# One GpSimd power for the squares of one group and the variances of another, in a macaron block on one core

## The reference

```python
x = x + 0.5 * ffn(layernorm(x), w_up, w_down)
x = x + attn(layernorm(x), Wf, Wi, Wh)
x = x + 0.5 * ffn(layernorm(x), w_up, w_down)

def ternary_linear(x, w):
    alpha = mean(abs(w))
    w_t = sign(w) * (abs(w) > 0.5 * alpha)
    x_norm = x / (sqrt(sum(x * x)) / sqrt(d) + 1e-8)
    return x_norm @ w_t.T

ffn  = ternary_linear(gelu(ternary_linear(x, w_up)), w_down)      # 128 -> 512 -> 128
attn = h, with h[t] = sigmoid(Wf x[t]) * h[t-1] + sigmoid(Wi x[t]) * g(Wh x[t])   # written with logarithms
```

## Time and profile before

| What | Value |
|---|---|
| median of 3 runs | 262.69 us (262.29 to 263.86) |
| the profiled execution | 263.04 us |
| its span, first to last instruction | 261.3 us |
| mean granted TensorE clock | 0.991 of full speed |
| TensorE matmul busy | 236.6 us (91%) |
| VectorE busy | 234.1 us (90%) |
| ScalarE busy | 221.4 us (85%) |
| GpSimd busy | 216.4 us (83%) |
| DMA, over the span | 9.73 MB, mean 37 GB/s |

### The profile page before, as it was taken

One profiled execution on the slowest core, in us unless ns is written; L12 is line 12 of the kernel. 1 busy time (PEld: TensorE's weight loads), 2 busy tenths in 40 slices (PEclk: granted clock), 3 DMA queues, 4 the chain that ended last, 5 costly groups with the idle time before them and its releaser, 6 DMA issues.

```text
span 261.3 us, 9753 instructions
## 1 busy us (share of the span) xinstructions
PE 236.6 (91%) x3759; PEld 167.1 (64%) x3759; DVE 234.1 (90%) x754; ACT 221.4 (85%) x534; POOL 216.4 (83%) x400
## 2 busy tenths in 40 slices
PE   0759999999998899899999998679999999999992
PEld 0626777777777667655555544357777776777782
DVE  3798799999999998999999999986999999988784
ACT  2377999989998899879999997997899999999861
POOL 5676998989998898599999999998889989997133
PEclk9988999999999999999999999999999999999999
DMA  6990000000000000000000000000111211112114
GB/s 188 300 265 3 4 4 3 3 3 4 3 3 4 3 4 4 3 0 1 3 1 0 0 1 3 3 3 3 43 43 57 67 46 43 43 43 82 46 43 123
DMA packets 18062, 9.73 MB, mean 37 GB/s; under 512 B 608, under 2 KB 17888, under 8 KB 18016
## 3 DMA queue, kind: packets, MB, share of 16 engines
q1 hardware_dynamic: 17744, 8.98, 12.5%
q10 hardware_dynamic: 272, 0.13, 0.2%
HBM read 4.92 MB, written 4.19 MB: 35 GB/s over the span
## 4 chain that ended last, share of the span: by engine, by line
PE 53%; DVE 21%; ACT 7%; POOL 7%; issue 6%; DVEq 0%; ACTq 0%; POOLq 0%
PE Y L502 17%; PE U L458 9%; PE G L489 9%; PE U L459 8%; DVE hidden L701 5%; PE T L439 4%; ACT h_hi L330 4%; DVE st L719 3%; DVE h_lo L654 3%; PE U L518 2%; DVE cand L691 2%; DVE mv L619 2%; PE G L478 2%; POOL xn L236 2%; POOL root L212 2%
## 5 line engine op out<-in xcount | busy, mean ns | idle before, releaser
L654 DVE SCALAR_TENSOR_TENSOR h_lo<-h_hi,U 128x1024 f16<-128x1024 f16 x63 | 75.6, 1215 | 10.0 <-ACT h_hi L330 9.6
L324 ACT ACTIVATE U<-U 128x1024 f32<-128x1024 f32 x63 | 64.7, 1026 | 15.3 <-PE U L459 14.4
L236 POOL TENSOR_SCALAR xn<-X,neg_mean,rstd 128x128 f32<-128x128 f32 x156 | 67.8, 447 | 6.9 <-DVE rstd L624 4.2
L330 ACT ACTIVATE h_hi<-U 128x1024 f16<-128x1024 f32 x63 | 64.7, 1027 | 1.0
L502 PE MATMUL Y<-down_w,h_hi 128*128 128x128 f16 x496 | 59.4, 220 | 0.0
L502 PE MATMUL Y<-down_w_half,h_lo 128*128 128x128 f16 x496 | 59.0, 219 | 0.0
L458 PE MATMUL U<-xt_hi,up_w 128*128 128x512 f16 x128 | 49.2, 384 | 9.4 <-DVE h_lo L654 7.5
L212 POOL TENSOR_TENSOR root<-mv,half 128x8 f32<-128x8 f32 x31 | 51.0, 1644 | 2.3
L459 PE MATMUL U<-xt_lo,up_w 128*128 128x512 f16 x128 | 49.2, 384 | 0.0
L502 PEld LDWEIGHTS Y<-down_w_half,h_lo 128*128 128x128 f16 x496 | 48.5, 98 | 0.4
L502 PEld LDWEIGHTS Y<-down_w,h_hi 128*128 128x128 f16 x496 | 47.7, 98 | 1.6
(11 more groups left out here) (101 smaller groups left out, 415.2 us busy)
## 6 DMA issues: line engine op xcount, KB each, us to landing
X<-in_L_attn_x SPq DMA_DIRECT2D x16, 256.0 KB, 5.3
out_x<-X SPq DMA_DIRECT2D x15, 256.0 KB, 2.8
up_raw<-in_L_ffn_w_up SPq DMA_DIRECT2D x1, 256.0 KB, 4.5
down_raw<-in_L_ffn_w_down SPq DMA_DIRECT2D x1, 256.0 KB, 4.7
out_x<-X SPq DMA_DIRECT2D x1, 128.0 KB, 1.9
out_x<-X ACTq DMA_DIRECT2D x1, 128.0 KB, 2.9
gate_raw<-in_L_attn_Wh SPq DMA_DIRECT2D x1, 64.0 KB, 3.7
gate_raw<-in_L_attn_Wi SPq DMA_DIRECT2D x1, 64.0 KB, 3.6
```

The costliest lines, as they stand in the source:

```text
L236: m = eng.tensor_scalar(xn[:, n % 2, t, :], X[:, c, :], neg_mean[l][:, c:c + 1], rstd[l][:, c:c + 1], ALU.add, ALU.mult)
L324: eng.activation(U[part][:], U[part][:], ACT.Gelu, scale=1.0 / XN_SPLIT).then_inc(gelu_done, 1)
L330: eng.mul(h_hi[:, F % 2, 2 * part:2 * part + 2, :], U[part][:], H_SPLIT).then_inc(h_hi_done, 1)
L654: vec.scalar_tensor_tensor(out=h_lo[:, F % 2, 2 * part:2 * part + 2, :], in0=h_hi[:, F % 2, 2 * part:2 * part + 2, :], scalar=-1.0 / H_SPL ...
```

## The change

- **One power.** Where turn F of a feed-forward block still has a group five ahead of it (F + 5 in the same block), the sum of squares of F is written beside the variances of that group (`mv` column 3, already scaled by 4 / 512), and one GpSimd power takes all 12 values a partition (`ln_roots`); one addition makes both denominators (the floor of the fourth column is set once), and one reciprocal on VectorE both factors (`scale`). `rms_step`, `y_scale` and their instructions remain for the last five turns of either block.
- **Order on GpSimd and VectorE.** GpSimd's `ln_roots` of group k + 3 now stands before `norm` of k + 2, and the moments (`mv` column 2, `neg_mean`) before that, at the end of the turn before. VectorE's reciprocal stands between the two `h_lo` of turn k and takes group k + 3; statistics of group k + 4 stand after the adds.
- **Head.** Normalizing group 0 stands before the first weight limits; statistics of group 3, a first `h_lo` and the second ternary step are put in another order.
- **First turn's gates.** The gates of the first two turns of the recurrence stand before the gram and down of the last group, in other PSUM banks; the sum of squares of group 14 goes to VectorE; four tiles of statistics are taken out there and done in four later turns of five.
- **Start of the second feed-forward block.** The last add of the recurrence stands before the statistics.
- **End.** The last gram is done by columns between the rows of the down product before; the last adds wait for two rows of the down product at a time; the rows added by GpSimd are shared with VectorE, and their output goes in two DMAs.

The diff, cut to what the text speaks of:

```diff
+        def rides_with(F):
+            l, k = (0, F) if F < groups else (2, F - groups)
+            return (l, k + 5) if k + 5 < groups else None
+
+        def rider(l, g):
+            return None if g < 5 else g - 5 if l == 0 else g - 5 + groups
...
             def ln_roots(l, g):
-                if l == 0 or g >= BY_ACT:
-                    ln_moments(l, g)
+                F = rider(l, g)
+                w = 2 if F is None else 3
                 pool.wait_ge(var_set[l], 2 * (g if l == 0 else g + 1))
-                eng.tensor_tensor(root[l][:, g % 2], mv[l][:, cols(g), 1:3], half[:], ALU.pow).then_inc(root_done[l], 1)
+                if F is not None:
+                    pool.wait_ge(ssq_done, F + 1)
+                eng.tensor_tensor(root[l][:, g % 2, :, 0:w], mv[l][:, cols(g), 1:1 + w], half[:, :, 0:w],
+                                  ALU.pow).then_inc(root_done[l], 1)
...
+                if 2 <= k < groups - 3:
+                    ln_roots(0, k + 3)
+                elif groups - 3 <= k < groups:
                     rms_step(k - 2)
...
-                if k + 3 < groups:
-                    ln_roots(0, k + 3)
-                if 0 <= s - 28 < groups:
+                if k + 4 < groups:
+                    ln_moments(0, k + 4)
+                if 0 <= s - 28 < BY_ACT:
                     ln_roots(2, s - 28)
+                if 0 <= q < groups - 4:
+                    ln_moments(2, q + 4)
...
             def scales(l, g):
                 dve.wait_ge(den_done[l], g if l == 0 else g + 1)
-                vec.reciprocal(rstd[l][:, cols(g)], den[l][:, g % 2]).then_inc(rstd_done[l], 1)
+                if rider(l, g) is None:
+                    vec.reciprocal(scale[l][:, cols(g), 0], den[l][:, g % 2, :, 0]).then_inc(rstd_done[l], 1)
+                else:
+                    vec.reciprocal(scale[l][:, cols(g), :], den[l][:, g % 2]).then_inc(rstd_done[l], 1)
...
+            for k in range(2, groups):
+                if k + 1 < groups:
+                    low_part(k + 1)
+                if k == 2:
+                    scales(0, 4)
                 h_low(k, 0)
+                if 2 < k < groups - 3:
+                    scales(0, k + 3)
                 h_low(k, 1)
+                if k == 2:
+                    scales(0, 5)
+                if diagonal_by_max(k - 1):
+                    sum_squares(k - 1)
+                finish_ffn(k - 2)
+                if k + 4 < groups:
+                    stats(0, k + 4)
+                    mean_var(0, k + 4)
+                if k == groups - 1:
+                    candidate(0)
+                later_stats(k)
...
-                room = 0 if s < groups - 9 else 1 if s < groups - 5 else 4
+                room = 0 if s < groups - 9 else 1 if s < groups - 5 else 5 if groups + 3 <= s < groups + 7 else 4
...
+            turn(groups + 1)
+            for n in range(3):
+                gate(0, n)
+            gate(1, 0)
+            turn(groups + 2)
+            gate(1, 1)
+            gate(1, 2)
+            gram(groups - 1)
+            down(groups - 1)
+            turn_back(0)
...
+            down(LAST - 1, [0])
+            last_gram(0)
+            last_gram(1)
+            last_gram(2)
+            down(LAST - 1, [1])
+            last_gram(3)
+            down(LAST - 1, [2, 3])
+            down(LAST)
```

More of the change, by code:

```diff
@@ L145, in cols, with rstd, y_factor, y_ready @@
             return slice(g * TILES, g * TILES + n)
+        def rides_with(F):
[3 more added lines that the diff above has]
+            return None if g < 5 else g - 5 if l == 0 else g - 5 + groups
+        alone = [F for F in range(2 * groups) if not rides_with(F)]
+        def rstd(l, c):
+            return rstd1[:, c:c + 1] if l == 1 else scale[l][:, c, 0:1]
+        def y_factor(F, t):
+            if not rides_with(F):
+                return y_scale[:, F % 4, t:t + 1]
+            l, g = rides_with(F)
+            return scale[l][:, g * TILES + t, 1:2]
+        def y_ready(engine, F):
+            if rides_with(F):
+                l, g = rides_with(F)
+                engine.wait_ge(rstd_done[l], g + 1)
+            else:
+                engine.wait_ge(y_scale_done, alone.index(F) + 1)
         def by_both(n):
@@ L491, in gram, with products @@
-                m.then_inc(gram_done, 1)
+            def products(F, t, c, last):
+                for right in (h_hi, h_lo):
+                    for n in range(2):
+                        e = slice(t * P + n * HALF, t * P + (n + 1) * HALF)
+                        m = pe.matmul(gram_of(F)[n * HALF:(n + 1) * HALF, t, 0:HALF], h_hi[:, F % 2, c, e], right[:, F % 2, c, e],
+                                      start=False, stop=last and right is h_lo, tile_position=(0, n * HALF))
+                return m
@@ L493, in down, with last_gram @@
+            def last_gram(c):
+                pe.wait_ge(h_lo_done, 2 * LAST + max(c, 1))
+                if c == 0:
+                    mask(LAST)
+                for t in range(TILES):
+                    m = products(LAST, t, c, t == TILES - 1 and c == chunks - 1)
+                if c == chunks - 1:
+                    m.then_inc(gram_done, 1)
             def down(F, rows=range(TILES)):
@@ L771, in _ @@
+            scan(0)
+            candidate(1)
+            finish_ffn(groups - 2)
+            later_stats(groups + 1)
+            scan(1)
+            add_rnn(0)
+            finish_ffn(groups - 1)
+            candidate(2)
+            later_stats(groups + 2)
+            add_rnn(1)
+            for s in range(groups + 3, 2 * groups):
+                r = s - groups
                 if r == groups - 1:
                     low_part(groups)
[L773 to L774 removed]
```

348 lines of the change are left out of this document (206 added, 142 removed).

## The result

The changed kernel takes **271.13 us** (median of 4 runs, 270.70 to 271.72); the kernel before, beside it, 262.62 (262.29 to 263.86). The ratio is 1.0317, 95% interval [1.0283, 1.0352]: slower by 3.2%. The forecast was 270.6 us, with 264.3 to 275.0 as the range. The profiled execution took 271.72 us, with a span of 269.4 (before 263.04 and 261.3).

The account below looks back on a forecast made before the run. Several engines at once held a feed-forward turn, with TensorE's floor at 5.35 us; the new loop would exceed it. Terms summed to +7.95 on 263.04, 270.99, less 0.35 to the median: 270.6 us, range 264.3 to 275.

Parts of the forecast that it names:

- The loop: First feed-forward block: mv, power, reciprocal, h_lo, adds, statistics close once a turn, 6.78 us; nine periods cost +9.45 us.
- The power: GpSimd's merged root on 12 values takes 2.28 us, bounded by 1.644 and 2.65.
- The last leg: End of the first block's loop: the last such reciprocal delays the adds behind it, mv to adds 3.40 to 4.84, +1.45 us.
- The three turns after: First block's three turns after the loop run near the 5.35 floor, norm late in the first; -0.2 us together.
- Head: Kernel start up to mv of group 6: earlier h_lo, but root before norm of group 4; -0.5 us, between -1 and +0.5.
- First gates and middle: First recurrence gates start sooner, but VectorE carries the stage and gets another sum of squares; +0.4 us, between -1.2 and +1.5.
- Its turns: Second feed-forward block, no loop: nine turns fall from 5.53 to 5.38 us, -1.3 us (none to -1.6).
- End: Kernel end: last squares' products come some 0.8 us sooner, another add of rows on VectorE; -0.6 us (0 to -1.2).
- Relief: Rival: next group's mv ready a turn earlier, loop slack, both feed-forward stages at 5.38 us a turn; 256.6 us; chance 0.05.
- Cheap: Rival: GpSimd's power on 12 values costs what 8 do, loop 6.15 us a turn; 264.3 us; chance 0.10.
- dear power: Rival: GpSimd's power on 12 values takes 2.65 us, 3.7 us more in total; 274.3 us; chance 0.08.
- Clock: Rival: TensorE, pausing some 1.4 us in each slow first-block turn, falls to a low granted clock; 306 us; chance 0.03.

Follow-up runs that it names:

- the early statistics: Changed kernel with each group's first-layer statistics made one turn earlier on VectorE (group k+5 at the end of step k); 260.21 us, ratio 0.989.
- the root of 8: Changed kernel with the root on 8 values instead of 12, a constant replacing the power of the squares, all waits kept; 266.32 us, ratio 1.0091.
- norm first: Changed kernel with GpSimd's order in steps 2 to 12 turned, norm before the next group's moments and root; 272.78 us, ratio 1.0371.
- the first block unmerged: Changed kernel with power, reciprocal and statistics of the first feed-forward block as in the kernel before, the rest as changed; 262.34 us, ratio 0.9971.
- the further steps: Two edits on top of the early statistics: start reordered (259.73 us), then also recurrent-layer statistics spread one tile a turn over steps 3 to 10 (258.96 us).
- the earlier head: The early statistics plus norm of group 4 before the first root of 12, statistics of group 6 before the reciprocal of group 5; 259.73 us.
- the best version: The earlier head plus recurrent-layer statistics made one tile a turn from step 3 to 10, so no recurrent turn makes five; 258.96 us, ratio 0.9852.

## Why the prediction was right

The signs that it had named are there: VectorE idles 1.53 us before the reciprocal of 8 values with den as releaser, mv starts are 6.76 us apart, the root of 12 takes 2.28, TensorE's granted clock is 1.00, and the second block's turns take 5.43.

**The loop** (forecast +9.45 in nine periods of 6.78): +9.24, periods of 6.76. Its legs by the rows above: mv to GpSimd 0.47, to the root 0.56, root to den 2.35, to the reciprocal 0.24, to h_lo 0.12, h_lo 1.08, adds 1.04, statistics 0.90. Each was worked out from an instruction of the kernel before. That it is a loop, and not a long operation, is shown by the early statistics (same operations, no loop, 5.55 a turn); that the power is a leg of it, by the root of 8; that norm is none, by norm first.

**The power** (2.28, between 1.644 and 2.65): 2.28. The two rows gave it by a straight line.

**The last leg** (+1.45): +1.42. **The three turns after** (-0.2): +0.36. They take 6.10, 5.77 and 5.66 us; TensorE waits for xn in the first of them alone, 0.94 us, and what holds the others above the floor is not shown. **Head** (-0.5): -0.17; runs with the same head differ in it by 0.6 (adds of group 0 at 32.88 and 32.26), so this term was below what one execution can show.

**First gates and middle** (+0.4): -0.20 in the sum, but of larger parts than I gave: -2.42 up to the first scan, which I had capped at the 1.24 us of VectorE's gaps, then +1.01 and +1.21. The first does not hang on the first block's merge: from adds of group 13 to the first scan it is 5.54 us before, 3.12 in the changed kernel and 3.11 with the first block unmerged. No run undoes the gates' new place, so its cause is argued only. The last is the price of the statistics that I had called moved: turns of five tiles; spread out they cost nothing there.

**Start of the second block** (-0.75): -0.84, and 0.85 when undone. **Its turns** (-1.3, at 5.38): -0.88, at 5.43; a third of the forecast gain did not come. By the profile TensorE is busy 48.73 of the 48.89 us there, so it sets the turn, but at 5.43 and not at the 5.35 of the last four turns; why is not shown. **End** (-0.6): -0.83 in the span, 0.6 when only TensorE's order is undone.

**Around the span** I had carried over 1.74 us; the profiled execution had 2.32, and no trace says why. With +8.10 in the span, forecast 7.95, the sum came out near the result partly because errors of both signs met: the three turns, the second block's turns and the head were 0.56, 0.42 and 0.33 too good, the middle, the end and the loop 0.60, 0.23 and 0.21 too dear.

**The rivals.** *Relief* needed mv a turn earlier: the early statistics are just that, and gave 260.21, with the further steps 258.96, not the 256.6 of the rival; TensorE's 5.38 a turn was not reached in the first block (5.55 with the early statistics, 5.42 with the earlier head, 5.52 in the best version, which makes more statistics there). *Cheap* and *dear power* fell with 2.28. *Clock*: in nine turns with a TensorE pause of over 1.2 us each the granted clock stayed 1.00.

One reading of the prediction is of a single turn: the earlier trace rows is the tighter of two that alternate, and the next takes 5.73 us (mv at 38.55 and 44.28), with a wait of 0.30 us for h_hi. No term of the sum rests on its 5.34.

The Trainium skill (Perfetto Trace Analysis, section Optimizing Scalar/DVE Operations) says that grouping can help a saturated engine, and that broken-up instructions may finish sooner where ScalarE or VectorE are not saturated but hold other engines up. Here GpSimd's power was grouped, and the outcome has the sign of both halves: 0.11 us a turn gained in the second block, 1.2 lost in the first. But the fullest engine of the second block before was TensorE (49.25 of 49.77 us, GpSimd 44.39), and with the statistics a turn earlier the same grouped power left the first block's turns at 5.55 us, no longer than the 5.56 before: the order decided, not the grouping.

## What to carry to other kernels

Before two small operations are merged across groups, write down for the merged one which input was made last and which output is wanted first, and follow both round through the other engines' lists; if they close on themselves within a turn, add up the legs and compare the sum with the turn, not with busy time. Then look for the list entry that can move a turn ahead: here the same merge made the kernel 3.2% slower or 1.1% faster by the place of one line of statistics. A wait that is the longest on the busiest engine need not be the cause: take it away in one run and see whether the period moves.

## What the runs showed of the hardware

**The clock after the recurrence.** The second block starts with a stretch in which TensorE has little to do. With the order of the change it is the same in each run, and yet the granted clock (before the DMA share; PE busy alone) is not. The run with the first block unmerged, then the changed kernel, in windows of 2 us from the same place:

```profile
168.08:170.08 2.00, 0.79 (x5) 1.00 0.01 4
170.08:172.08 2.00, 0.91 (x3) 0.71 0.00 0
172.08:174.08 2.00, 2.00 (x8) 0.50 0.00 0
174.08:176.08 2.00, 2.00 (x70) 0.94 0.00 0
```

```profile
177.69:179.69 2.00, 0.79 (x5) 1.00 0.02 8
179.69:181.69 2.00, 0.91 (x5) 1.00 0.00 0
181.69:183.69 2.00, 1.58 (x11) 1.00 0.00 0
```

After 0.79 and 0.91 us of work in two windows, with TensorE waits of 0.77 and 1.53 us in both runs, the one falls to 0.50, that is 1.2 GHz, for about 3 us, and the other stays at 2.4 GHz. It fell in four of the eleven profiles with this order, and cost 0.9 to 1.1 us (20.75 to 20.93 us from the scan of turn 14 to the first adds, against 19.82 to 19.85). In two kernels the time of an execution goes with its mean granted clock: the one with the first block unmerged takes 261.03 to 262.18 us at 0.997 and above, 263.34 to 263.98 at 0.978; the best version 258.44 to 258.96 at 0.997 and above, 260.49 and 260.70 at 0.985 and 0.984. The clock is not all of it: the kernel before has an execution of 263.45 us at 1.000 and one of 262.80 at 0.993. Differences under 1 us are therefore read here from traces, stretch by stretch.

The Trainium skill (TensorE: Matmul & The Clock Gate, section HAM oscillation) tells of a kernel whose waits for data throw the array back to the low clock in every round. The pauses here, 1.24 us in every turn, are shorter than those waits and never did; this one lull, with no longer pause than 1.53 us, did so in four of eleven profiles.

I tried to fill the lull:

```diff
             up(groups, 1)
+            pe.wait_ge(rnn_added, groups - 1)
+            for _ in range(3):
+                pe.matmul(G[:].rearrange("p t d -> p (t d)"), up_w[:, 0:P], xt_hi[:, 0, :], start=True, stop=True)
             turn_back(groups - 1)
+            for _ in range(6):
+                pe.matmul(Y[:, 0].rearrange("p t d -> p (t d)"), up_w[:, 0:P], xt_hi[:, 0, :], start=True, stop=True)
```

> The run with the early statistics, the mended head and the spread statistics, with nine matmuls added between the recurrent stage and the second block, into PSUM that is overwritten afterwards: three before the last turn_back, six behind it, so that TensorE has hardly a pause there. Nothing is left out, the added products are not used. In four of the ten profiles the granted clock fell to 0.50 just there, after some 4 us with TensorE busy under half of the time, and the stretch from the last but one scan to the first adds took 20.8 to 20.9 us instead of 19.85. Theory E (the pause lets the clock fall, by chance from run to run): the clock stays 1.00 there in the profile, the fastest time stays as it was (258.4), the slow ones go, median 258.3 to 258.8. If the pause has nothing to do with it: the spread stays (258.4 to 260.7); if the added matmuls stand in the way, 0.3 to 1 us slower throughout.

Measured: 259.35 us (259.22 to 260.20), ratio 0.9867 [0.9849, 0.9884], where the base has 0.9852 [0.9825, 0.9879]; the hoped-for 258.3 to 258.8 did not come. The profile shows the clock at 1.00 in the stretch and 19.85 us for it, so the matmuls hold nothing up there; but the base's own profile shows the same, and two of the four executions still have a mean clock of 0.991. It stays open whether the added work keeps the clock up there, and where those two lost it.
